# A graph transformer layer on one core: the last head's probabilities transposed by VectorE and a passage through DRAM, with own PSUM banks and an earlier order for the tail

## What is computed

```python
x = x + gnn(layernorm(x), edges, ...)     # attention over edges, skip product, layer norm
x = x + ffn(layernorm(x), ...)            # a small MLP per row, adds 2.0 at two one-hot places

# gnn, for each head h
alpha = (q[dst] * k[src]).sum(-1) / sqrt(512)
attn  = softmax of alpha over the edges of each dst
agg   = segment_sum(attn * v[src], dst)
x_lin = (agg + x @ Wskip + bskip) @ Wlin + blin ; h = x_lin + x_attn[:, :512]
return gamma * (h - mean) / sqrt(var + 1e-5) + beta

# ffn, for each row: nibbles decoded from columns 16:80 (x > 0.5, argmax), three MLPs with
# 160 hidden units (and, or, xor), one chosen by columns 1..3, result rounded and clipped
# to 0..15, active only where column 0 >= 0.5; then row = row + normalised row + one-hot
```

## Time and profile before

| what | value |
|---|---|
| runs | 1041.16 us median of 3 (1040.66 to 1042.87) |
| profiled execution | 1043.38 us, of which the span from first to last instruction is 1041.7 us |
| PE | 1007.2 us busy, 97% of the span |
| DVE | 578.8 us, 56% |
| ACT | 334.2 us, 32% |
| POOL | 90.0 us, 9% |
| mean granted clock of TensorE | 0.987 of full |

### The profile page before, as it was taken

The page is one execution under the profiler, slowest core; times in us unless marked ns, Lnnn a source line. Parts: engine busy times, 40 slices in busy tenths (PEclk is TensorE's granted clock), DMA queues, the critical chain, the costliest instruction groups (busy, mean ns, idle before and its releaser), DMA issues.

```text
span 1041.7 us, 13311 instructions
## 1 busy us (share of the span) xinstructions
PE 1007.2 (97%) x4913; PEld 823.8 (79%) x4913; DVE 578.8 (56%) x1350; ACT 334.2 (32%) x499; POOL 90.0 (9%) x256
## 2 busy tenths in 40 slices
PE   6999999999999999999999999999999999999993
PEld 4777677678888888888888888888888888877872
DVE  6999897442455445235455532645454245557586
ACT  4445554102223323123233211422233132434342
POOL 2112101000000000000000000000000000323244
PEclk9999999999999999999999999999999999999996
DMA  9755555400152253006233410442352011000011
GB/s 319 271 203 177 217 178 182 159 31 0 52 182 73 80 165 112 7 1 207 76 97 80 157 52 1 122 136 76 101 159 73 1 33 34 21 21 31 31 39 38
DMA packets 36569, 104.04 MB, mean 100 GB/s; under 512 B 4240, under 2 KB 19978, under 8 KB 33180
## 3 DMA queue, kind: packets, MB, share of 16 engines
q1 hardware_dynamic: 31900, 86.41, 26.4%
q0 software_dynamic: 4608, 16.78, 4.1%
HBM read 64.17 MB, written 39.00 MB: 99 GB/s over the span
## 4 chain that ended last, share of the span: by engine, by line
PE 86%; DVE 7%; issue 3%; ACT 1%; DMA 1%; POOL 1%; SPq 0%; DVEq 0%; ACTq 0%
PE ps_o L1301 9%; PE ps_o L1302 9%; PE ps_o L1303 9%; PE ps_r L1301 8%; PE ps_r L1302 8%; PE ps_r L1303 8%; PE ps_s L1302 8%; PE ps_s L1303 8%; PE ps_s L1301 8%; PE ps_t L1301 2%; PE ps_t L1302 2%; PE ps_t L1303 2%; DVE onehot_src L875 1%; DVE opnd_lo L865 1%; PE ps_s L1401 1%
## 5 line engine op out<-in xcount | busy, mean ns | idle before, releaser
L1301 PE MATMUL ps_s<-xT_hi,tT 128*128 128x512 f32 (+1 forms) x480 | 169.6, 353 | 0.0
L1302 PE MATMUL ps_s<-xT_lo,tT 128*128 128x512 f32 (+1 forms) x480 | 168.7, 351 | 0.0
L1303 PE MATMUL ps_s<-xT_hi,tT 128*128 128x512 f32 (+1 forms) x480 | 168.6, 351 | 0.0
L1301 PE MATMUL ps_o<-y,pT 128*128 128x512 f32 x400 | 156.6, 391 | 0.0
L1302 PE MATMUL ps_o<-y,pT 128*128 128x512 f32 x400 | 156.2, 391 | 0.0
L1303 PE MATMUL ps_o<-y,pT 128*128 128x512 f32 x400 | 155.9, 390 | 0.0
L828 ACT ACTIVATE prob<-prob,nbias 128x1250 f32<-128x1250 f32 x40 | 53.7, 1342 | 281.3 <-DVE nbias L1260 281.3
L1252 DVE CUSTOM_DVE_ANT_0 prob<-ps_s,maskb 128x1250 f32<-128x1250 f32 x40 | 58.2, 1455 | 133.7 <-issue 133.6
L1302 PEld LDWEIGHTS ps_s<-xT_lo,tT 128*128 128x128 f32 x480 | 90.7, 189 | 13.6
L1301 PEld LDWEIGHTS ps_s<-xT_hi,tT 128*128 128x128 f32 x480 | 90.6, 189 | 13.5
L1303 PEld LDWEIGHTS ps_s<-xT_hi,tT 128*128 128x128 f32 x480 | 90.7, 189 | 12.8
(11 more groups left out here) (245 smaller groups left out, 1717.3 us busy)
## 6 DMA issues: line engine op xcount, KB each, us to landing
regrouped<-prob SPq DMA_DIRECT2D x120, 160.0 KB, 2.8
whole<-regrouped SPq DMA_DIRECT2D x30, 640.0 KB, 3.9
products<-prod_parts POOLq DMA_DIRECT2D x32, 512.0 KB, 3.7
gbuf<-products SPq DMA_DIRECT2D x4, 2048.0 KB, 9.5
mbuf<-products SPq DMA_DIRECT2D x4, 2048.0 KB, 9.1
stage<-in_Wskip SPq DMA_DIRECT2D x4, 1024.0 KB, 5.7
stage<-in_Wq SPq DMA_DIRECT2D x3, 1024.0 KB, 8.8
stage<-in_Wk SPq DMA_DIRECT2D x3, 1024.0 KB, 6.2
```

Of the source, the lines that this page charges most:

```text
L1301: nc.tensor.matmul(out_, a[0], b[0], start=start, stop=False)
L1302: nc.tensor.matmul(out_, a[0], b[1], start=False, stop=False)
L1303: return nc.tensor.matmul(out_, a[1], b[0], start=False, stop=stop)
```

## The change

1. The last head uses `turn`, `regroup`, `whole_high` and `whole_low` as the others do; `transposes`, `pt_high` and `pt_low` are gone.
2. `hidden` writes to `ps_hid`, the two banks of `ps_t`, with semaphores of its own (`hid_done`, `hid_free`). The transposed features go to the free end of the third bank of `ps_s`.
3. The tail's steps stand one to two iterations sooner: in iteration d centre and residual of tile d-2, features of d-3, hidden of d-4 (PE) and, on DVE, `dots` and `results` of d-3 at the end. PE has no iterations behind the tenth: outputs of tiles 8 and 9 follow at once.
4. `split_w1` stands at the end of iteration 1 instead of 2; on SP the five loads of the tail stand behind `regroup` of tiles 0 and 1.
5. `features` ends in one multiplication of 108 columns instead of three of 36.

```diff
 # SP
+            for d in range(2):
+                regroup(H - 1, d)
             sp.wait_ge(rot_done, rot(H - 1, LAST_Y + 1))
             sp.dma_start(gamma_bc[0:R, :], gamma.partition_broadcast(R)).then_inc(tail_in, 16)
...
+            load_x(0)
             sp.wait_ge(w1_ready, 1)
-            for t in range(2):
-                load_x(t)
-            for d in range(3, NT + 5):
-                if d - 5 >= 0:
-                    store(d - 5)
-                if d - 1 < NT:
-                    sp.wait_ge(res_ready, d - 2)
-                    load_x(d - 1)
+            load_x(1)
+            for d in range(2, NT):
+                if d >= 4:
+                    store(d - 4)
+                regroup(H - 1, d)
+                sp.wait_ge(res_ready, d - 1)
+                load_x(d)
+            for t in range(NT - 4, NT):
+                store(t)
 # POOL
+            add_beta(0)
+            for d in range(2, NT):
+                if d >= 3:
+                    choice(d - 3)
+                    gates(d - 3)
+                add_beta(d - 1)
+                h_factor(d - 2)
+                z_factors(d - 2)
+            add_beta(NT - 1)
+            h_factor(NT - 2)
+            choice(NT - 3)
+            gates(NT - 3)
+            z_factors(NT - 2)
+            h_factor(NT - 1)
+            choice(NT - 2)
+            gates(NT - 2)
+            z_factors(NT - 1)
+            choice(NT - 1)
+            gates(NT - 1)
 # DVE
+            def last_head(h):
+                for t in range(NT - 2):
+                    rotating_lo(h, t, "y", t)
+                for d in range(NT):
+                    peaks(h, d)
+                    if d >= 3:
+                        features(d - 3)
+                    weigh(h, d)
+                    turn(h, d)
+                    for local, g, half in side_fills(True, d):
+                        rotating_lo(h, local, "t", (g, half, h))
+                    if d < 2:
+                        rotating_lo(h, fill["y", NT - 2 + d], "y", NT - 2 + d)
+                    if d >= 2:
+                        add_out(h, d - 2, True)
+                    if d >= 1:
+                        whole_low(h, d - 1)
+                    if d == 1:
+                        split_w1()
+                    if d >= 2:
+                        centre(d - 2)
+                        residual(d - 2)
+                    if d >= 3:
+                        dots(d - 3)
+                        results(d - 3)
+                add_out(h, NT - 2, True)
+                centre(NT - 2)
+                whole_low(h, NT - 1)
+                features(NT - 3)
+                residual(NT - 2)
+                dots(NT - 3)
+                results(NT - 3)
+                add_out(h, NT - 1, True)
...
+            def dots(t):
+                for r in range(2):
+                    dve.wait_ge(hid_done, 2 * t + r + 1)
+                    nc.vector.scalar_tensor_tensor(out=ps_hid[r], in0=ps_hid[r], scalar=0.0, in1=w2_bc[0:R, :],
+                                                   op0=ALU.max, op1=ALU.mult,
+                                                   accum_out=s_sel[t % 2][:, r:r + 1]).then_inc(hid_free, 1)
 # PE
+            def last_head(h):
+                pe.wait_ge(m_in, 16 * (h + 1))
+                for t in range(NT - 2):
+                    values(h, t, t)
+                for d in range(NT):
+                    scores(h, d, [0])
+                    if d >= 4:
+                        hidden(d - 4)
+                    scores(h, d, [1, 2])
+                    for local, g, part_ in side_fills(True, d):
+                        score_side(h, local, g, part_)
+                    if d < 2:
+                        values(h, fill["y", NT - 2 + d], NT - 2 + d)
+                    if d >= 2:
+                        outputs(h, d - 2, {NS - 1: d - 3} if d >= 3 else {})
+                outputs(h, NT - 2, {}, {1: NT - 4})
+                outputs(h, NT - 1, {5: NT - 3}, {8: NT - 3})
+                for t in range(NT - 2, NT):
+                    turn_features(t)
+                    hidden(t)
```

More of the change, by code:

```diff
@@ L1280, in head @@
                     if d < 2:
[L1281 to L1283 removed]
+                        rotating_lo(h, fill["y", NT - 2 + d], "y", NT - 2 + d)
                     if 2 <= d < NT + 2:
[L1285 to L1288 removed]
+                        add_out(h, d - 2, False)
@@ L1289, in head @@
+                    if 0 <= d - 1 < NT:
                         whole_low(h, d - 1)
-                    if last and d == 2:
-                        split_w1()
+            def last_head(h):
+                for t in range(NT - 2):
+                    rotating_lo(h, t, "y", t)
+                for d in range(NT):
+                    peaks(h, d)
+                    if d >= 3:
+                        features(d - 3)
+                    weigh(h, d)
+                    turn(h, d)
+                    for local, g, half in side_fills(True, d):
+                        rotating_lo(h, local, "t", (g, half, h))
+                    if d < 2:
+                        rotating_lo(h, fill["y", NT - 2 + d], "y", NT - 2 + d)
+                    if d >= 2:
+                        add_out(h, d - 2, True)
+                    if d >= 1:
+                        whole_low(h, d - 1)
+                    if d == 1:
+                        split_w1()
+                    if d >= 2:
+                        centre(d - 2)
+                        residual(d - 2)
+                    if d >= 3:
+                        dots(d - 3)
[8 more added lines that the diff above has]
+                add_out(h, NT - 1, True)
+                centre(NT - 1)
+                residual(NT - 1)
+                features(NT - 2)
+                features(NT - 1)
+                dots(NT - 2)
+                results(NT - 2)
+                dots(NT - 1)
+                results(NT - 1)
@@ L1494, in values, with scores @@
                 ins.then_inc(rot_done, 1)
-            def scores(h, d, cols, last):
+            def scores(h, d, cols):
                 n = NT * h + d
@@ L1546, in outputs @@
                 for t in range(NS):
-                    if last and t == PT_GROUPS[2][0]:
-                        pe.wait_ge(pt_free, PE_TURNED + 3 * d + 4)
-                    if not last and t == HALVES[1][0]:
+                    if t == HALVES[1][0]:
                         pe.wait_ge(pt_free, 2 * n + 3)
-                    if t == 3 and hid is not None:
-                        hidden(hid)
+                    if t in turns:
+                        turn_features(turns[t])
+                    if t in hids:
+                        hidden(hids[t])
                     ins = mm3(ps_o[:, :], [pT[:, s, t, :] for s in range(2)],
@@ L1565, in _, with head @@
             pe.wait_ge(count_final, 1)
-            def head(h, last):
+            def head(h):
                 pe.wait_ge(m_in, 16 * (h + 1))
@@ L1569, in head @@
                     values(h, t, t)
[L1570 removed]
+                for d in range(NT + 2):
                     if d < NT:
[L1572 to L1594 removed]
```

393 lines of the change are left out of this document (166 added, 227 removed).

## The result

The changed kernel took 1030.54 us (median of 4 runs, 1030.35 to 1033.56) beside 1040.91 us for the kernel before on the same chip: a ratio of 0.9899, 95% interval 0.9884 to 0.9913. A later repeat gave 1031.50 us (4 runs, ratio 0.9906, interval 0.9879 to 0.9933). The prediction was 1030.7. The profiled execution took 1030.69 us, with a span of 1029.0 us.

What follows compares the result with a forecast made beforehand. PE, busy 97% of the span, was taken as the bound. The span of 1041.7, less 11.4 up to the last scores, plus 0.9 behind, gave 1031.2 us; by the median 1041.16 - 10.5 = 1030.7, range 1026.5 to 1036.

Steps and rivals of the forecast that it cites:

- The transposes: Last head, up to the end of its last scores: taking the transposes off PE removes 8.7 us there.
- A: The moment when the last head's last scores end; the stretch up to it was forecast at 127.1 us against 138.49.
- The stall at the start: PE waits before scores of tile 3 for late loads and the weights' split: 4.0 us, plus 1.7 of slow clock.
- Own banks take the stalls away: Before the side fills of iterations 5 and 7: separate banks remove two stalls of 2.16 us and the slow clock behind.
- VectorE between: Iterations from d = 4: VectorE's work of 13.8 us fits PE's 14.1 by 0.3; 0.6 of lateness allowed.
- The third rival: VectorE's iteration grows to 14.5 to 15 us through GpSimd: 3 to 5 us more, 1033 to 1037; chance 0.16.
- Behind A: From the last scores to the end: 49.8 us against 48.93, with stalls before outputs of tiles 8 and 9.
- one slow stretch for each long stall: Last head: three slow-clock stretches, each behind a stall longer than 2.16 us, costing 1.7 us each.

Runs made afterwards that it cites:

- the first experiment: The five loads of the tail's parameters issued between the DRAM passages of tiles 0 and 1 instead of behind both, against the changed kernel: 1022.07 us.
- the edits of the end: Against the changed kernel, tile 9's low parts moved sooner on VectorE (1030.42 us), or also with early loads and GpSimd's factors ahead of its gates (1024.34 us).
- late sums and shared banks: Against the changed kernel, weighted sums and results put back behind the next maximum and hidden products back in the two rotating PSUM banks: 1045.80 us.

## Why the prediction was right

- **The transposes** were the term that carries it: 8.7 us of the stretch up to A and 11 of the whole. Put back, they cost 8.6 us up to A and 10.2 of the whole by the medians.
- **The stall at the start** was laid out from distances of head 2 as 4.0 us (2.5 to 7) and measured 5.58. Two rows were mis-sized: the weights took 6.9 us from issue to landing, not 5.06 with up to 1 more, and the split 4.83 us, not 4.11, since its first copy ran beside GpSimd's addition. The slow clock behind it cost 2.5 us, not 1.7. Together this is the step with the largest error, 2.4 us, and the first experiment shows its whole price, 8.2 us.
- **Own banks take the stalls away**: the stalls and the slow clock behind them (7.7 us) did go, but the cause that the prediction named is only one of two. The sums, done ahead of the next maximum, do it without the banks, and by the medians they are worth more than the banks; that the total came out right does not bear out the prediction's account of this term.
- **VectorE between**: the prediction had it fit by 0.3 us and allowed 0.6 of lateness at A. Iterations are 14.17 us apart, as TensorE alone needs; before each maximum from tile 4 on VectorE still idled 0.4 to 0.7 us. The third rival, VectorE late through GpSimd, did not show; its collisions did, at the start and in the edits of the end.
- **Behind A**: 49.8 forecast, 47.4 measured. The stall before the outputs of tile 8 was 1.79, not 3.1 (the first half of its low parts was done at A + 8.8, not 10.0: VectorE was not late, and its features took 2.0 us, not 2.4); that before tile 9 was 2.80 for 2.7; one slow stretch came, not two.
- The errors were +2.8 up to A (129.9 for 127.1) and -2.4 behind it. They cancel; the 0.2 us of agreement in the total is luck within about 3 us. The span forecast beside it, 1031.2 us, was 2.2 above the measured 1029.0, for the profiled execution began its last head 2.6 us sooner.

## What to carry to other kernels

When a queue gets new work ahead of old loads, look at who waits for the last of those loads and what stands behind that waiter in its list: here five loads behind one DMA passage held a maximum, and TensorE for 5.6 us with a slow clock on top. Issuing the loads 8.6 us sooner was worth nearly as much again as the change (8.5 and 10.4 us by the medians). Look also at what is loaded behind that waiter: moving the split later moved a load of x with it, and in the trace VectorE stood still for that. A stall that two edits could each have removed should be tested as a square of four before one of them gets the credit. Where a profile shows a shorter stall, check that the end came sooner too: a slow stretch ahead of it can have taken it up.

## What the runs showed of the hardware

**The clock behind short stalls is not settled by their length.** Behind the stall at the start (5.04 to 6.37 us, nine profiles) it always fell. Behind a stall of 1.7 to 1.8 us before the outputs of tile 8 it fell in three of eleven profiles, behind one of 2.2 to 2.9 us before those of tile 9 in four of twelve, and never behind both in one profile. Yet it fell behind each of the five stalls of 2.0 to 2.7 us further up in the head (two in the kernel before, two with late sums and shared banks, one with the split late), and behind both of 3.6 us before the outputs of tile 8 (a clock of 0.53 to 0.71 in the stretches behind these seven). The changed kernel fell behind the first of the pair. Its repeat, by windows at the outputs of tiles 8 and 9, behind the second:

```profile
991.40:997.00 5.60, 5.53 (x24) 4.59 (x25) 4.51 (x14) 1.26 (x5) 2.69 (x6) 1.00 0.69 187
...
1001.80:1007.00 5.20, 5.16 (x16) 4.07 (x17) 2.90 (x11) 0.81 (x1) 4.05 (x15) 0.67 0.00 0
```

With the same two stalls, A to the end took 47.2 to 47.4 us where it fell (48.7 once), and 45.7 to 45.8 where it fell behind neither, so one slow stretch cost about 1.6 us. The prediction's count of one slow stretch for each long stall was wrong. It had set that beside the Trainium skill, "TensorE: Matmul & The Clock Gate", by which the gate's window runs free; identical code falling at different places agrees with it.

**GpSimd waits for VectorE too.** The prediction priced only VectorE held by GpSimd. In the changed kernel's timeline:

```profile
985.69 1.45 DVE L1152 CUSTOM_DVE_ANT_0 prob<-prob,count 128x1250 f32<-128x1250 f32 x1
...
985.73 1.46 POOL L614 TENSOR_TENSOR ones<-ones 128x1 f32<-128x1 f32 x1
987.26 0.19 POOL L615 TENSOR_TENSOR ones<-ones,b_bc 128x3 f32<-128x3 f32 x1
...
1021.19 0.19 POOL L614 TENSOR_TENSOR ones<-ones 128x1 f32<-128x1 f32 x1
```

An operation on one column, 0.19 us at the quiet end of the kernel, took 1.46 us beside VectorE's multiplication of two SBUF operands and ended with it, and so it did in each of iterations 3 to 9. The Trainium skill, "SBUF — State Buffer", section "SBUF: two separate sides", describes such a lock; this row agrees with it in the direction that I had not priced. It cost nothing here, because VectorE reads what GpSimd makes of it only in `results`, some 6 us after GpSimd is done.
